# Gated attention and expert block on one core: sums of y and inverse deviations moved to free PSUM columns, x in two buffers, statistics and normalisation in other slots, and no hand-over through SyncE at the end

## The reference

```
x1  = x  + tanh(g_xattn) * attention(layernorm(x), ctx)     # 16 heads of 32, causal, projections Wq Wk Wv Wo, bias bo
out = x1 + tanh(g_ffn)   * ffn(layernorm(x1))               # 8 experts, the best 6 of each row weighted, and one shared MLP

layernorm(x) = (x - mean) / sqrt(var + 1e-5)                # over the 512 numbers of a row
attention    = (softmax(mask(q k^T / sqrt(32))) v) Wo^T + bo
```

## Time and profile before

| | |
|---|---|
| median of 3 runs | 1872.62 us (1871.63 to 1873.6) |
| time of the profiled execution | 1871.45 us |
| its span, first to last instruction | 1869.7 us |
| busy share of PE, PEld, DVE, ACT, POOL over the span | 95%, 80%, 76%, 52%, 50% |
| from 100 to 540 us: busy PE, DVE, ACT, POOL | 415.45, 346.14, 365.93, 326.61 of 440 us |
| mean granted clock of PE | 0.989 |

### The profile page before, as it was taken

How to read it: one execution, slowest core, us unless ns; L and a number is a source line. 1 busy time by engine, 2 the same in 40 slices (tenths; PEclk the granted TensorE clock), 3 DMA queues, 4 the chain that set the end, 5 groups by cost and what they waited for, 6 DMA issues and landing times.

```text
span 1869.7 us, 33758 instructions
## 1 busy us (share of the span) xinstructions
PE 1785.5 (95%) x11904; PEld 1488.6 (80%) x11904; DVE 1420.5 (76%) x3101; ACT 963.3 (52%) x2260; POOL 926.1 (50%) x1185
## 2 busy tenths in 40 slices
PE   6899999999996899999999999999999999999999
PEld 6788878878885678888778888877888887888887
DVE  6777877887777677777977777788777788777776
ACT  5888888888887424333533343443333444333331
POOL 4776777777667433433533344444343453333330
PEclk9999999999996999999999999999999999999999
DMA  4778888877886412121141221123212112211111
GB/s 149 139 148 171 145 169 163 167 158 152 175 165 141 145 57 69 56 71 54 34 158 46 79 68 57 46 78 115 79 46 79 45 57 99 93 46 56 46 46 45
DMA packets 301000, 182.84 MB, mean 98 GB/s; under 512 B 210080, under 2 KB 265376, under 8 KB 300832
## 3 DMA queue, kind: packets, MB, share of 16 engines
q1 hardware_dynamic: 300832, 180.69, 38.7%
HBM read 111.43 MB, written 18.87 MB: 70 GB/s over the span
## 4 chain that ended last, share of the span: by engine, by line
PE 69%; DVE 15%; issue 6%; ACT 4%; POOL 3%; DMA 2%; SPq 1%; DVEq 0%; POOLq 0%; ACTq 0%
PE gate_up L1292 32%; PE down L1807 19%; PE bank L789 13%; DVE ops_lo L1149 2%; DVE acc L1658 2%; ACT probs L597 2%; POOL hidden L1506 1%; PE scores L895 1%; DVE y L677 1%; DVE x_in L641 1%; PE y_values L917 1%; DVE stats L621 1%; PE rows_t L779 1%; PE y_values L915 1%; DVE y_sum L673 1%
## 5 line engine op out<-in xcount | busy, mean ns | idle before, releaser
L1292 PE MATMUL gate_up<-xo_hi,ops_hi 128*128 128x512 f32 x1120 | 440.6, 393 | 13.0 <-DVE hidden L1268 4.5
L1292 PE MATMUL gate_up<-xo_hi,ops_lo 128*128 128x512 f32 x1120 | 436.7, 390 | 0.0
L1292 PE MATMUL gate_up<-xo_lo,ops_hi 128*128 128x512 f32 x1120 | 436.5, 390 | 0.0
L487 POOL TENSOR_TENSOR halves<-probs,halves 128x384 f16<-128x384 f32 x244 | 226.7, 941 | 85.5 <-ACT halves L591 84.4
L1658 DVE SCALAR_TENSOR_TENSOR acc<-down,scale,acc 128x512 f32<-128x512 f32 x320 | 238.5, 746 | 34.8 <-PE down L1807 34.3
L1292 PEld LDWEIGHTS gate_up<-xo_hi,ops_hi 128*128 128x128 f32 x1120 | 210.5, 188 | 66.5 <-DVE gated L1268 9.6
L597 ACT ACTIVATE probs<-probs,neg_max 128x128 f32<-128x128 f32 (+1 forms) x512 | 229.0, 449 | 56.8 <-DVE neg_max L719 56.8
L1506 POOL TENSOR_TENSOR hidden<-hidden,gated 128x512 f32<-128x512 f32 x120 | 157.4, 1319 | 189.8 <-DVE hidden L1273 170.4
L1807 PE MATMUL down<-d_hi,h_hi 128*128 128x512 f32 x640 | 249.1, 389 | 0.0
L1807 PE MATMUL down<-d_hi,h_lo 128*128 128x512 f32 x640 | 249.0, 389 | 0.0
L1807 PE MATMUL down<-d_lo,h_hi 128*128 128x512 f32 x640 | 249.0, 389 | 0.0
(11 more groups left out here) (182 smaller groups left out, 4240.3 us busy)
## 6 DMA issues: line engine op xcount, KB each, us to landing
g_raw<-in_w_gate SPq DMA_DIRECT2D x40, 512.0 KB, 3.5
u_raw<-in_w_up SPq DMA_DIRECT2D x40, 512.0 KB, 3.5
d_raw<-in_w_down SPq DMA_DIRECT2D x40, 512.0 KB, 3.4
c_in<-in_ctx_t SPq DMA_DIRECT2D x16, 512.0 KB, 4.5
x_in<-in_x SPq DMA_DIRECT2D x16, 512.0 KB, 6.0
x_res<-in_x SPq DMA_DIRECT2D x16, 512.0 KB, 4.9
x_between<-x_res SPq DMA_DIRECT2D x16, 512.0 KB, 3.4
acc<-x_between SPq DMA_DIRECT2D x32, 256.0 KB, 4.0
```

The lines of the kernel that those rows point to most:

```text
L487: pool.tensor_tensor(halves[k % HALVES][:, 1, :], probs[k % RING][:], halves[k % HALVES][:, 0, :], ALU.subtract).then_inc(p_lo_made, 1)
L1292: ins = pe.matmul(gu_ps[bank][:], ops[x][:, which, a, c, :], xo[y][:, b, c, :], start=(begins and c == 0 and i == 0), stop=(c == CH - 1 an ...
```

## The change

It has five parts.

1. **`y_sum` in PSUM.** The four scores banks become one tensor `scores`; the sums of `close_group` go to columns 0 to 127 of its banks 0 and 1 (`y_sum_ps`), and the product reads them there. The last two groups of the last batch keep the SBUF tile. Since these columns share banks with the scores, `group_scores` gets a wait: the scores of group number G (counted through all batches) wait until group G-3 is closed (`y_made`).
2. **`rstd` in PSUM.** `normalise` first copies `rstd` (128x2) to columns 0 and 1 of scores bank 3, then normalises by a `scalar_tensor_tensor` whose second tensor is that column, broadcast. The scores of the first group of an iteration wait until x is normalised (`xn_made`).
3. **Two buffers for x.** Batches with an even number go to the new tile `x_odd`, others to `x_in`. The load of slot 3 moves to slot 1, ahead of `x_res`, and waits for the transposes of two batches before instead of one.
4. **Slots.** `statistics` moves from slot 7 to 5, POOL's Newton steps stay in slot 7, `normalise` moves from slot 10 to 13.
5. **The seam.** `early_free` is gone: ACT and POOL wait for `scores_done` and `v3_made` themselves. In iteration 16 the store of `x_res` moves from slot 0 to slot 2, behind the turn of slot 1.

```diff
+    x_odd = sb("x_odd", [P, T, D])
+    def x_of(n):
+        return x_in if n.k % 2 else x_odd
...
-    sc_ps = [psum(f"scores{j}", [P, P + 3 * P]) for j in range(JH)]
+    scores = psum("scores", [P, JH, P + 3 * P])
+    sc_ps = [scores[:, j, :] for j in range(JH)]
+    rstd_ps = scores[:, JH - 1, 0:T]
+    y_sum_ps = scores[:, 0:T, 0:P].rearrange("p t (h d) -> p t h d", d=DH)
...
-    RES_LOAD, X_LOAD, C_LOAD, GATE_LOAD, ROWS_LOAD = 2, 3, 9, 12, 13
-    LN_SLOT, XN_SLOT = 7, 10
+    X_LOAD, RES_LOAD, C_LOAD, GATE_LOAD, ROWS_LOAD = 1, 2, 9, 12, 13
+    LN_SLOT, NEWTON_SLOT, XN_SLOT = 5, 7, 13
...
+    def is_tail(b, g):
+        return b.k == B - 1 and g >= H // JH - 2
...
-                    if s == 0 and has(i, -2):
+                    if s == (2 if is_end(i) else 0) and has(i, -2):
...
-                    if s == 1 and is_last(i):
-                        sp.wait_ge(v3_made, T * B)
-                        sp.wait_ge(scores_done, H * (B - 1))
-                        sp.sem_inc(early_free, 1)
...
-                        sp.wait_ge(xt_done, ln.times(T))
-                        sp.dma_start(x_in[:], row(x_v, ln)).then_inc(x_loaded, DMA)
+                        wait(sp, xt_done, ln.times(T, -T))
+                        sp.dma_start(x_of(ln)[:], row(x_v, ln)).then_inc(x_loaded[ln.k % 2], DMA)
...
-                    if s == places(i).moments and has(i, 2):
+                    if s == (NEWTON_SLOT if i.k >= 0 else places(i).moments) and has(i, 2):
                         inverse_std(ln)
...
                 dve.wait_ge(rstd_made, ln.times(1, 1))
+                wait(dve, xn_made, ln.times(T))
+                dve.tensor_copy(rstd_ps, rstd[:]).then_inc(rstd_kept, 1)
+                dve.wait_ge(rstd_kept, ln.times(1, 1))
                 for t in range(T):
-                    dve.tensor_scalar(x_in[:, t, :], x_in[:, t, :], mv[:, t, 0:1], rstd[:, t:t + 1],
-                                      ALU.subtract, ALU.mult).then_inc(xn_made, 1)
+                    dve.scalar_tensor_tensor(out=x_of(ln)[:, t, :], in0=x_of(ln)[:, t, :], scalar=mv[:, t, 0:1],
+                                             in1=rstd_ps[:, t:t + 1].to_broadcast([P, D]), op0=ALU.subtract,
+                                             op1=ALU.mult).then_inc(xn_made, 1)
...
-                dve.tensor_reduce(y_sum[:], y_ps[:].rearrange("p t h x d -> p (t h) d x"), AX.X,
+                whole = y_sum[:].rearrange("p (t h) d -> p t h d", t=T) if is_tail(b, g) else y_sum_ps
+                dve.tensor_reduce(whole, y_ps[:].rearrange("p t h x d -> p t h d x"), AX.X,
                                   ALU.add).then_inc(group_chain, 1)
...
+                if g == 0 and has(i, 1):
+                    pe.wait_ge(xn_made, i.times(T, 2 * T))
+                wait(pe, y_made, i.times(H // JH, g - H // JH + 2))
...
         if (phase, s) == (1, 1):
-            act.wait_ge(early_free, 1)
+            act.wait_ge(scores_done, H * (B - 1))
+            act.wait_ge(v3_made, GROUPS * B)
             weights_hi(act, 0, (W_A,))
```

More of the change, by code:

```diff
@@ L115 @@
     pv_done: object
-    early_free: object
+    v3_made: object
 class Slots(NamedTuple):
@@ L211, in attention @@
     even = heads_of(0)
-    sb("experts_space", [P, 2 * JH * C * S - D])
+    x_odd = sb("x_odd", [P, T, D])
+    sb("experts_space", [P, 2 * JH * C * S - D - T * D])
+    def x_of(n):
+        return x_in if n.k % 2 else x_odd
     v_rest = [sb("v_rest0", [P, D])]
@@ L255, in attention @@
     bank = [psum(f"bank{i}", [P, D]) for i in range(2)]
-    sc_ps = [psum(f"scores{j}", [P, P + 3 * P]) for j in range(JH)]
+    scores = psum("scores", [P, JH, P + 3 * P])
+    sc_ps = [scores[:, j, :] for j in range(JH)]
     y_ps = psum("y_values", [P, T, JH, 2, DH])
     rows_ps = psum("rows_t", [P, D])
+    rstd_ps = scores[:, JH - 1, 0:T]
+    y_sum_ps = scores[:, 0:T, 0:P].rearrange("p t (h d) -> p t h d", d=DH)
     x1_stored, x1t_stored, x1_made, x_hat_made, hat_t_made, scores_done, o_done, v_done = done[:8]
-    q_done, xt_done, c_lo_made, max_made, pv_done, early_free = done[8:]
+    q_done, xt_done, c_lo_made, max_made, pv_done, v3_made = done[8:]
     row_chain, guess2_made, pool_chain2 = sem("row_chain"), sem("guess2_made"), sem("pool_chain2")
@@ L267, in attention @@
     small_loaded = sem("small_loaded")
-    x_loaded, c_loaded, res_loaded = sem("x_loaded"), sem("c_loaded"), sem("res_loaded")
+    x_loaded, c_loaded, res_loaded = [sem("even_x_loaded"), sem("odd_x_loaded")], sem("c_loaded"), sem("res_loaded")
     ident_made, mask_made, bias_made = sem("ident_made"), sem("mask_made"), sem("bias_made")
-    pool_chain, rstd_made, v3_made = sem("pool_chain"), sem("rstd_made"), sem("v3_made")
+    pool_chain, rstd_made = sem("pool_chain"), sem("rstd_made")
     res_made = sem("res_made")
@@ L286, in attention @@
     yt_lo_made = sem("yt_lo_made")
-    y_made = sem("y_made")
+    y_made, rstd_kept = sem("y_made"), sem("rstd_kept")
     k_done, yt_done, hat_t_done = sem("k_done"), sem("yt_done"), sem("hat_t_done")
@@ L386, in sync @@
                 if n == 1:
-                    sp.dma_start(x_in[:], x_v[0]).then_inc(x_loaded, DMA)
+                    sp.dma_start(x_of(At(0, 2, 0))[:], x_v[0]).then_inc(x_loaded[0], DMA)
                     sp.dma_start(gates[:, 0:1], g_xattn.partition_broadcast(P)).then_inc(small_loaded, DMA)
@@ L435, in run @@
                     if s == X_LOAD and has(i, 2):
-                        sp.wait_ge(xt_done, ln.times(T))
-                        sp.dma_start(x_in[:], row(x_v, ln)).then_inc(x_loaded, DMA)
-                    if s == X_LOAD and phase(i) == 2:
+                        wait(sp, xt_done, ln.times(T, -T))
+                        sp.dma_start(x_of(ln)[:], row(x_v, ln)).then_inc(x_loaded[ln.k % 2], DMA)
+                    if s == 3 and phase(i) == 2:
                         start.sync(sp, phase(i), 1)
@@ L617, in statistics @@
             def statistics(ln):
-                dve.wait_ge(x_loaded, ln.times(DMA, DMA))
+                dve.wait_ge(x_loaded[ln.k % 2], DMA * (ln.k // 2 + 1))
                 for t in range(T):
-                    dve.bn_stats(stats[:, t, :], x_in[:, t, :]).then_inc(norm_chain, 1)
+                    dve.bn_stats(stats[:, t, :], x_of(ln)[:, t, :]).then_inc(norm_chain, 1)
                 dve.wait_ge(norm_chain, ln.times(NORM_STEPS, T))
@@ L677, in close_group @@
                 dve.tensor_tensor(y[:, part, :, at:at + P].rearrange("p t (h d) -> p t h d", d=DH),
-                                  y_sum[:].rearrange("p (t h) d -> p t h d", t=T),
+                                  whole,
                                   row_inv[:].rearrange("p h t -> p t h").unsqueeze(3).to_broadcast([P, T, JH, DH]),
@@ L837, in units @@
                             pe.wait_ge(xt_lo_made, n.times(T, 1))
-                        transpose_rows(lambda c: x_in[:, t, c * P:(c + 1) * P], rows_ps).then_inc(xt_done, 1)
+                        transpose_rows(lambda c: x_of(n)[:, t, c * P:(c + 1) * P], rows_ps).then_inc(xt_done, 1)
                     if s in places(i).q:
@@ L1375, in start_gpsimd @@
         elif (phase, s) == (1, 3):
-            pool.wait_ge(early_free, 1)
+            pool.wait_ge(scores_done, H * (B - 1))
+            pool.wait_ge(v3_made, GROUPS * B)
             x_lo_by(pool, 0, B11)
```

## The result

The changed kernel takes 1856.11 us (median of 4 runs, 1851.14 to 1859.34) against 1873.11 for the kernel before (4 runs); ratio 0.9907, interval 0.9888 to 0.9927. That is 17 us faster. The forecast was 1847 with a range of 1837 to 1862: right in direction and in the range, 9 us short in size. The profiled executions differ by 16.8 us (spans 1869.7 and 1852.9).

A forecast was written before the change was run, and what follows sets the result against it. PE was taken as the bound, busy nearly throughout, so only its waits could be won. 19.5 us (thirteen iterations) + 0.4 (iteration 14) - 0.5 (start) + 6 (seam) = 25.4 us, giving 1847 us, range 1837 to 1862.

The forecast's parts named there:

- The old waits: PE's waits on `q_lo` (slot 10) and `t_lo` (slot 12), 0.9 and 1.3 us an iteration, would both go.
- The new wait of the slot-8 scores: Scores of slot 8 would wait for y, 0.7 us an iteration, bounds 0.35 and 1.2.
- one small instruction lost to POOL: Statistics in slot 5 would take 2.35 us: the 2.55 measured less what one small instruction lost to POOL.
- the rival on x: x lands after 7 us or more, so slot 8 waits above 1.5 us: 1858 to 1864 us, chance 0.14.
- The start: Iteration 0's scores wait until batch 1 is normalised: 0.5 us lost, bounds 0 and 2.3.
- The seam: Hand-over removed and last turn ahead of the store of x: 6 us gained, bounds 2 and 9.
- The last turn: In iteration 16 it no longer follows the store of x: up to 3.5 us, 2.7 taken.
- The hand-over: ACT's 4.88 us idle before its cast goes; some 1.6 come back, 3.3 gained, bounds 1 and 4.9.
- The product in PSUM: Product of y reading PSUM would take its least, 0.43 us, without spread; it took up to 1.52.
- the slower rival: Sum written to PSUM and read back costs more; 28 us slower, 1900 us, at 1.5 us a closing; chance 0.05.
- the step that takes relief of DVE for a condition of the gain: Product of y and normalisation lose time to POOL's SBUF work; without PSUM relief only 10 us gained in all.
- PSUM operands do not relieve DVE: Product stays 1.52 us in slot 6, normalisation 1.14; new wait 1.8, 10 us gained, 1862 us; chance 0.08.

The follow-up runs named there:

- ysum_sbuf_res8: res_slot_8 with the sum of y back in SBUF and without the scores' wait on it: 1839.73 us.
- res_slot_8: The changed kernel with POOL's addition of the bias to `x_res` moved from slot 6 to slot 8: 1844.14 us.
- again: The changed kernel run a second time, without an edit: 1854.9 us.
- x_early: The changed kernel with x of batch i+3 loaded in slot 6 of iteration i, and batch 1 ahead of the loop: 1846.9 us.
- start: The changed kernel with batches 0 and 1 normalised in the old form, so iteration 0's scores wait for nothing: 1851.84 us.
- combined: ysum_sbuf_res8 with the edit of start (batches 0 and 1 normalised in the old form): 1834.9 us.
- store_first_res8: res_slot_8 with the store of x1 back in slot 0 of iteration 16, ahead of the last turn: 1845.93 us.
- slots_alone: The changed kernel with old normalisation and sum of y in SBUF, without PE's waits on them: 1844.71 us.
- slots_back: The changed kernel with statistics in slot 7, normalisation in slot 10 and SBUF without the scores' wait on it; sum of y stays in PSUM: 1854.12 us.
- rstd_sbuf_res8: res_slot_8 with the old SBUF normalisation in slot 13, without the scores' wait on it; sum of y stays in PSUM: 1867.24 us.

## Why the prediction was right, and where it was off

**The old waits** were read rightly: 0.9 + 1.3 us an iteration, both gone. The period of ordinary iterations fell from 35.8 to 33.7, by 2.1 us; without the new wait it is 33.4 (ysum_sbuf_res8), so the old waits were worth 2.4 where I read 2.2, if nothing else in the iteration changed.

**The new wait of the slot-8 scores** was set at 0.7 and is 0.27 in an ordinary iteration (33.68 in res_slot_8 against 33.41 in ysum_sbuf_res8), below its lower bound of 0.35. The reason is x: it landed after 4.2/4.5/6.0 us (12 loads from 100 us on) where I took 6.0, so the statistics wait in only two of the thirteen iterations. By this term alone the forecast would have been 5.6 us too small.

**The long iterations** are the step that failed. I summed an ordinary iteration thirteen times, with `var_eps`, `shifted` and `rstd` at their undisturbed length, and wrote off what "one small instruction lost to POOL". Slot 5 puts these three shortly before POOL's pair on `x_res`, and the new wait ties PE to what stands behind them. In the profiled execution the three long iterations cost 9.0 us: 5.9 the one with `x_res` (and a late x), 1.45 the one with POOL's `halves`, 1.65 the one with a late x alone. The last is the rival on x in a single iteration, at a landing of 5.7 us. That meeting `x_res` is the larger part is borne out by res_slot_8 (9.0 us less over the thirteen than after and 4.3 less than again), that a late x isn't needed by x_early. How the gain of res_slot_8 divides between fewer meetings and a timelier x is not shown. The two errors nearly cancel: 19.5 us were forecast for the thirteen, and 26.9 less 9.0 were measured. That the sum came out within 2 us is luck.

The earlier trace rows showed the same thing on other instructions, and I took it for a reason for the change, not for a danger to it. The Trainium skill (SBUF — State Buffer, section Who interferes with whom) says that VectorE and GpSimd share a pair of SBUF ports, which one instruction holds to its end, and names `tensor_scalar` and two-input `tensor_tensor` from SBUF among those that can contend for it. The trace agrees: `rstd` at 1.19 us ended with POOL's instruction, the normalisation of 3.61 us outlasted `c_lo`, and the forms with a PSUM operand never varied. By that rule every small `tensor_scalar` in the moved piece could be held up, whatever its size, where I had looked at the large ones alone. Even `half_var`, 0.15 us elsewhere, took 1.28 us beside `x_res` in start.

**The start** is the mis-sized term that decided the total: 0.5 us forecast, with 2.3 as the bound; 6.15 measured, some 4.3 of them by the new wait. I put scores and one K projection (2.3 us) behind the wait for x. In the trace after they take 4.3 us from the scores to the transposes, and the first scores 0.80 us instead of 0.50: behind the wait of 5.05 us PE's granted clock was low, where before it was full. The stretch from 38 to 41 us, which has 1.00 before, reads now:

```profile
38.00:41.00 3.00, 1.74 (x25) 1.54 (x25) 2.25 (x3) 0.00 (x0) 0.58 (x1) 0.53 0.00 0
```

That the wait on the normalisation is what costs is shown by start (4.3 us back) and again by ysum_sbuf_res8 against combined (74.25 and 70.28).

The other 1.9 us need not be the change's. Batch 1 is normalised later after (the copy starts at 37.51, before the normalisation started at 35.65), because PE's work from 24.5 to 27.5 us ran at half the clock. The kernels of store_first_res8 and res_slot_8 are the same up to iteration 16, and have both levels there:

```profile
24.50:27.50 3.00, 3.00 (x8) 2.28 (x8) 0.69 (x1) 0.14 (x1) 0.90 (x1) 0.52 0.52 180
```

```profile
24.50:27.50 3.00, 3.00 (x18) 2.59 (x17) 0.78 (x2) 0.83 (x3) 0.89 (x1) 1.00 0.55 180
```

In both PE had idled 2.09 us before the transposes at 23.4. So one kernel gets either, and the mark of iteration 1 moves with it (75.22 and 73.93). After reads 0.50 in this stretch and before 1.00, while start, in the old form, reads 0.50 too.

Of the 8.6 us by which the profiled execution falls short of the forecast's 25.4, the start is 5.65, the thirteen iterations 1.6, the seam 0.5 (iteration 14's 0.4 counted with it) and the rest 0.85.

**The seam** came out at 5.9 for 6 (6.4 with iteration 14), but its terms did not, and the sum is again partly luck. The last turn is worth 2.3 us of the 2.7, but only 0.9 of it by the later landing; the rest fits the low clock behind PE's wait. The hand-over is worth 1.35 of the 3.3. I let 1.6 us come back for the scores' wait on y, and more came back, but that wait is not shown to be the reason. PE waited 3.13 and 5.06 us for y in iteration 15 (scores at 561.53 and 569.97), yet it waited for the same y before, 3.05 and 4.43 us at later instructions, and the kernels without the scores' wait have the same seam (slots_alone 90.14, ysum_sbuf_res8 90.45). What else covers ACT's idle time stays open. The parts undone singly sum to 3.65 of 6.5 us between before and res_slot_8; the other 2.9 belong neither to the slots (slots_back 90.20) nor to the PSUM operands (slots_alone 90.14). Whether they show only when both parts are undone wasn't tried.

**The product in PSUM** was costed rightly (0.42, 0.744, a copy of 0.16 for the 0.3 assumed), and a sum written to PSUM is hardly dearer (0.647 us against 0.640), so the slower rival never began. But the step that takes relief of DVE for a condition of the gain is refuted: slots_alone has the gain without. The rival "PSUM operands do not relieve DVE" kept the scores' new waits, and with the wait on y relief does count (rstd_sbuf_res8 is 23 us slower than res_slot_8). What the prediction lacked is the plainer kernel without the PSUM operands and without the waits that they bring: they relieve DVE, and the gain doesn't need it.

## What to carry to other kernels

When a run of small instructions is moved ahead of something that PE waits for, look at what the neighbour engine does at that time and take the longest duration in the trace, not the commonest: an instruction on two columns of data cost up to 1.3 us here. Moving the neighbour's work by two slots was worth 11 us, more than half of what the change itself gave. Try each part of a change without the others: here the slots alone beat the whole by 10 us, since the PSUM operands brought waits of their own. And when a buffer moves to where it needs a new wait, price that wait at the start of the loop too, where nothing is ahead.

## What the runs showed that I had not expected

- A DVE `tensor_scalar` of 128x2 takes 0.17 us alone and up to 1.28 beside POOL's 128x512 addition (`half_var` in start); one of 128x512 takes 0.53 alone and up to 2.8 beside POOL's 128x1024 subtraction. A DVE instruction of the same size with a PSUM operand stays at 0.74 to 0.75.
- After a wait of PE of 3.5 us the granted clock was 0.50 (1.2 GHz) for the next 4 us and 0.73 in the mean of the 3 us behind them, so that a wait cost more than its length: the longest iteration lost 5.9 us on a wait of 3.5. After a wait of 2.09 us, the same code ran at 0.52 in one execution and at 1.00 in another.
- Two changes, each worth 15 to 19 us over the thirteen iterations by itself (the sum in PSUM, the moved slots), are worth 18 together (22.5 in again). The second x buffer is in all of them.
